# A two-layer attention network on one core: the first layer's attention probabilities transposed in three blocks across heads instead of four, one per head

## The chip, the cores and the metric

The kernel runs on one NeuronCore of a Trainium2 chip. The metric is the device time of one execution in microseconds (us); the median of three runs of the kernel before is 2927.92 us (2922.82 to 2928.58). TensorE is called PE, VectorE DVE, ScalarE ACT, GpSimd POOL and SyncE SP, as in the profile.

## What is computed

Two layers, each a cross attention followed by a feed-forward part, on x of 8 batches x 512 tokens x 512 features. The change touches only the attention of the first layer:

```python
# x: (8, 512, 512), ctx_1024: (8, 77, 512); 16 heads of 32 features
q = (layernorm(x) @ Wq + bq)          # heads of 32
k = (ctx @ Wk + bk)
v = (ctx @ Wv + bv)
scores = einsum('bqhd,bkhd->bhqk', q, k) / sqrt(32)
scores = where(mask, -1e9, scores)
probs  = softmax(scores, axis=-1)     # over the 77 keys
ctx    = einsum('bhqk,bkhd->bqhd', probs, v)
x = x + ctx @ Wo + bo
```

Every product of the attention is made in float32 accuracy from two float32r parts: a matrix is split in a high part (rounded to float32r by ACT) and a low part (the rest, by DVE), and a product is hi x hi + lo x hi + hi x lo, three matmuls into one PSUM bank (`product`, lines 117 to 121).

## The kernel before

The program is a sequence of stages: the first layer (`build_layer0`, to about 680 us), its slots and latents, the second layer's attention, and its experts. Only `build_layer0` is changed.

In it, a **group** s is 4 heads (HC = 4, 128 features) of one batch: s = 4b + c, with c from 0 to 3 (C = 4), so there are G = 32 groups. Batch b has 512 tokens, NT = 4 tiles of 128. The order of work is written by hand: each engine has its own loop over steps s, and engines meet only through semaphores (`pe_s`, `act_s`, `dve_s`, `pool_s`; `mark` counts, `after` waits), so each engine works strictly in its written order. The PSUM banks are placed by the table `place` (line 347), and `claim` (line 353) makes PE wait until the last reader of a bank's former unit has marked it free.

Step s of PE's loop (lines 644 to 691), in this order:

- `scores(s+1, tiles 0 to 2)`: per tile three float32r matmuls of 312 columns and one for the mask (line 571). The scores of tile t go to bank (4s + t) % 3, so tile 3 goes to the bank of tile 0 and waits for DVE to have read that one (`shift`, line 869)
- `probabilities(s, 0)` and `(s, 1)`: the normalised probabilities of one head, 128 tokens x 77 keys, are transposed tile by tile (line 611), four transposes per head into one bank, 77 rows x 512 tokens
- `scores(s+1, tile 3)`, then `queries(s+2)`: 12 matmuls
- `read_out(s, 0)`, `probabilities(s, 2)`, `read_out(s, 1)`, `probabilities(s, 3)`: a read-out is the product of one head's values (stationary) with its transposed probabilities (moving, 512 columns), three matmuls
- work of other batches, by c: c = 0 two tiles of `output(b-1)` (24 matmuls) and `logits(b-2)`; c = 1 the other two tiles of `output(b-1)` and 16 transposes of the next batch's x (line 558); c = 2 `weights_and_sums(b-2)` and 16 transposes for the feed-forward part; c = 3 `hidden(b-1)` (24 matmuls)
- `read_out(s, 2)`, `read_out(s, 3)`

The four read-outs of a group accumulate in one bank (bank 5). The values lie in `Vd`, which is zero but for the head's own 32 columns: head n reads columns n*(P-HD) to n*(P-HD)+128, so that each head adds only to its own 32 output rows. SP fills `Vd` in `values(s)` (lines 385 to 391): 4 heads x 2 parts = 8 DMAs of 77 rows x 32 columns. `values` is called for the groups 0 to 3 before SP's loop, and in step s for group s-1+C once the read-outs of group s-1 are done. `keys(b)` (line 378) loads the keys in 8 DMAs. In the step c = 1 SP also loads the x of batch b+2 into `xa` (line 432); the first such load comes right behind the four calls of `values` ahead of the loop.

ACT copies each transposed head's high part (`probabilities_hi`, line 714), DVE makes its low part (`probabilities_lo`, line 853, recorded at line 805), both of 77 rows x 512. `PT` holds two (high, low) pairs of buffers, and the transposes alternate between banks 3 and 4.

DVE's step (lines 872 to 982) is: `maximum` and `shift` of the four score tiles of s+1 with the low parts of the output of s-1 and of the heads 0 and 1 between them, the low part of the queries, the row sums (line 907, after ACT's exp) and their reciprocal, `probabilities_lo` of heads 2 and 3, and then by c: c = 0 low parts for and work on the routing logits (lines 916, 923, 950 to 962); c = 1 the residual of two output tiles (923), the low parts of the next batch's x, the routing weights (931 to 939) and the statistics; c = 2 low parts for the feed-forward; c = 3 `measure` of the next batch's x, which waits for the DMA into `xa` (line 979). POOL multiplies all of a group's exponentials by their reciprocals at once (line 508).

## Time and profile before

| | |
|---|---|
| median of three runs | 2927.92 us (2922.82 to 2928.58) |
| the profiled execution | 2931.27 us |
| its span | 2929.5 us |
| mean granted clock | 0.957 |
| PE busy | 2664.5 us, 91% |
| DVE busy | 2036.7 us, 70% |
| ACT busy | 1532.9 us, 52% |
| POOL busy | 1522.8 us, 52% |
| from 180 to 560 us: PE, DVE, ACT, POOL busy of 380 | 363.7, 293.0, 160.8, 195.1 us |

The profile is one execution, 1.8 us shorter in its span than in its own time and 3.4 us above the median. The time of a matmul in it includes a modelled end that overlaps the next one, so what a matmul costs in a row of them is read from start to start. A value in brackets behind a row is the idle time of the engine before it and what ended it.

### The profile page before, as it was taken

The numbers are of one execution on the slowest core, as the hardware profiler recorded it, in microseconds if no ns is written. First come the engines' busy times: TensorE is split into PE (matmuls) and PEld (weight loads), VectorE is DVE, ScalarE is ACT, GpSimd is POOL, SyncE is SP. The second block draws the span as 40 slices with busy tenths as digits, with TensorE's granted clock in tenths as the row PEclk, the third lists the DMA queues.
The fourth block names the chain that finished last, engine by engine and source line by source line (L and its number), as shares of the span: only waits on it lengthen the run. The fifth ranks groups of instructions, "written<-read, shape, count | busy, mean of one in ns | idle before, by whom it ended". The sixth has DMA issues, their size and how long they took to land. (4 is left out here: it accounts for less than half of the span.)

```text
span 2929.5 us, 41389 instructions
## 1 busy us (share of the span) xinstructions
PE 2664.5 (91%) x14790; PEld 2217.7 (76%) x14790; DVE 2036.7 (70%) x4037; ACT 1532.9 (52%) x2929; POOL 1522.8 (52%) x1149
## 2 busy tenths in 40 slices
PE   6799999986778699999999999999999999799698
PEld 5687887863435588888888888888888887677476
DVE  3677777742546377777777777777777777577656
ACT  2344344421213377777777777777777777111175
POOL 2355544320000166666666666666666666465555
PEclk9899999997888799999999999999999999899899
DMA  5222222123348633334333243332433314668475
GB/s 186 57 54 56 56 56 57 41 95 128 115 154 316 226 79 81 109 76 121 78 79 110 76 121 78 79 110 75 121 78 79 108 51 135 207 240 282 158 277 186
DMA packets 211758, 351.15 MB, mean 120 GB/s; under 512 B 75071, under 2 KB 81602, under 8 KB 203863
## 3 DMA queue, kind: packets, MB, share of 16 engines
q1 hardware_dynamic: 192771, 284.88, 32.7%
q0 software_dynamic: 11680, 45.02, 4.1%
q10 hardware_dynamic: 7104, 18.61, 1.6%
q8 instruction: 118, 1.93, 0.3%
q14 instruction: 85, 0.70, 0.1%
HBM read 172.47 MB, written 156.64 MB: 112 GB/s over the span
## 5 line engine op out<-in xcount | busy, mean ns | idle before, releaser
L1873 POOL TENSOR_SCALAR pa_Pr<-pa_Pr,pa_rs 128x590 f32<-128x590 f32 x512 | 902.0, 1768 | 487.7 <-DVE pa_rs L2102 487.5
L2106 DVE TENSOR_REDUCE pa_least<-pa_S 128x1 f32<-128x590 f32 x512 | 390.4, 762 | 230.6 <-PE pa_S L1937 228.5
L2027 ACT ACTIVATE pa_Pr<-pa_S,pa_least 128x590 f32<-128x590 f32 x512 | 385.0, 752 | 99.4 <-DVE pa_least L2106 96.2
L2059 DVE TENSOR_TENSOR pa_PTl<-pa_W,pa_PTh 128x512 fp32r<-128x512 f32 (+1 forms) x640 | 420.9, 683 | 20.3 <-ACT pa_PTh L1998 16.0
L1998 ACT ACTIVATE pa_PTh<-pa_W 128x512 fp32r<-128x512 f32 (+1 forms) x640 | 366.6, 595 | 59.2 <-PE pa_W L1948 47.6
L1948 PE MATMUL pa_W<-pa_ident,pa_Pr 128*128 128x128 f32 (+1 forms) x2560 | 370.8, 276 | 0.6
L1948 PEld LDWEIGHTS pa_W<-pa_ident,pa_Pr 128*128 128x128 f32 (+1 forms) x2560 | 303.3, 142 | 30.5 <-POOL pa_Pr L1873 2.9
L1964 PE MATMUL pa_O<-pa_PTh,pa_V 128*128 128x512 f32 (+1 forms) x640 | 289.5, 452 | 17.1 <-DVE pa_PTl L2059 12.8
L1965 PE MATMUL pa_O<-pa_PTl,pa_V 128*128 128x512 f32 (+1 forms) x640 | 253.2, 396 | 0.0
L1935 PE MATMUL pa_S<-pa_U,pa_Qh 128*128 128x296 f32 (+1 forms) x1024 | 228.8, 305 | 7.4 <-ACT pa_Pr L2027 0.4
L1935 PEld LDWEIGHTS pa_S<-pa_U,pa_Qh 128*128 128x128 f32 x1024 | 183.2, 188 | 55.4 <-ACT pa_Pr L2027 21.2
L1937 PE MATMUL pa_S<-pa_Um,pa_Ql 128*128 128x296 f32 (+1 forms) x1024 | 222.9, 299 | 0.0
L508 POOL TENSOR_TENSOR l_E<-l_E,l_rs 128x1232 f32<-128x1232 f32 x32 | 84.7, 2646 | 200.9 <-DVE l_rs L909 200.9
L1937 PEld LDWEIGHTS pa_S<-pa_Um,pa_Ql 128*128 128x128 f32 x1024 | 166.4, 189 | 0.0
L1964 PEld LDWEIGHTS pa_O<-pa_PTh,pa_V 128*128 128x128 f32 (+1 forms) x640 | 121.4, 190 | 44.2 <-DVE pa_PTl L2059 35.4
L119 PE MATMUL pa_W<-Wkv_hi,pa_z_hi 128*128 128x256 f32 x512 | 144.7, 283 | 0.0
L121 PE MATMUL pa_W<-Wkv_hi,pa_z_lo 128*128 128x256 f32 x512 | 144.2, 282 | 0.0
L120 PE MATMUL pa_W<-Wkv_lo,pa_z_hi 128*128 128x256 f32 x512 | 144.1, 281 | 0.0
L2553 ACT ACTIVATE ex_xT_hi<-ex_bank 128x512 fp32r<-128x512 f32 x92 | 53.0, 599 | 142.2 <-PE ex_bank L2449 135.9
L1965 PEld LDWEIGHTS pa_O<-pa_PTl,pa_V 128*128 128x128 f32 (+1 forms) x640 | 123.0, 192 | 5.2
L119 PE MATMUL pa_W<-pa_z_hi,Wq_hi 128*128 128x512 f32 x256 | 107.2, 419 | 18.6 <-DMA pa_z_lo<-z_s 18.6
L1998 ACT ACTIVATE pa_U<-pa_W 64x512 fp32r<-64x512 f32 x128 | 75.7, 592 | 90.1 <-PE pa_W L121 88.5
(503 smaller groups left out, 6647.5 us busy)
## 6 DMA issues: line engine op xcount, KB each, us to landing
xs_s<-pa_Ql SPq DMA_DIRECT2D x57, 576.0 KB
pa_Um<-pa_U SPq DMA_DIRECT2D x128, 147.5 KB
pa_Qh<-pa_Qh SPq DMA_DIRECT2D x128, 128.0 KB
o_s<-pa_O_hi SPq DMA_DIRECT2D x64, 256.0 KB, 2.0
o_s<-pa_O_lo SPq DMA_DIRECT2D x64, 256.0 KB, 2.3
Wkv_hi<-o_s SPq DMA_DIRECT2D x8, 2048.0 KB, 11.2
Wkv_lo<-o_s SPq DMA_DIRECT2D x8, 2048.0 KB, 16.7
l_xa<-x SPq DMA_DIRECT2D x8, 1024.0 KB, 6.4
```

The lines of the kernel that those rows point to most:

```text
L119: pe.matmul(out, a[0], b[0], start=first, stop=False)
L121: return pe.matmul(out, a[1], b[0], start=False, stop=last)
L1873: pool.tensor_scalar(p, p, rs[:, g % 2, t:t + 1], None, ALU.mult).then_inc(*pool_s.mark("probs", n))
L1935: pe.matmul(out[:, a0:a1], qh, U[p % 2][x][:, a0:a1], start=True, stop=False)
L1937: m = pe.matmul(out[:, a0:a1], ql, Um[p % 2][x][:, a0:a1], start=False, stop=True)
L1948: m = pe.transpose(bank_of[u][0:KEYS[c], t * P:(t + 1) * P], Pr[g % 2][:, t, c * P:c * P + KEYS[c]], ident[:, :])
L1964: pe.matmul(Oc[:, :], v, PTh[0:n, r, :], start=(c == 0), stop=False)
L1965: pe.matmul(Oc[:, :], v, PTl[0:n, r, :], start=False, stop=(c == NC - 1)).then_inc(*pe_s.mark("PV", g, c))
L1998: act.activation(out, src, ACT.Copy, scale=scale).then_inc(*act_s.mark("hi", *name))
L2027: act.activation(Pr[g % 2][:, t, :], scored[n % 2], ACT.Exp, scale=-1.0, bias=least[:, g % 2, t:t + 1], accum_out=rs[:, g % 2, t:t + 1]).t ...
L2059: dve.tensor_tensor(out, src, f32(hi_ap), ALU.subtract).then_inc(*dve_s.mark(*name))
L2106: dve.tensor_reduce(least[:, g % 2, t:t + 1], scored[n % 2], AX, ALU.min).then_inc(*dve_s.mark("least", n))
```

## The change

The probabilities of a group lie in SBUF as 4 heads x 77 keys = 308 adjacent columns per token tile. They are now cut without regard to heads into NK = 3 blocks of 128, 128 and 52 columns (`ROWS`). `PT` of a block has 128 (or 52) rows, and the values in `Vd` are laid out to match: row r of block k is key column 128k + r, and holds the 32 values of its head in that head's columns, zeros elsewhere. A read-out covers a block, not a head. So `values` has to cut the heads at the block edges: `pieces` has 6 parts (77, 51, 26, 77, 25 and 52 rows). The third block has two matmuls in place of three: its low part is written by DVE to rows 64 to 115 under the high part in rows 0 to 51 of the same buffer, and the high values are loaded a second time for these rows, so that one product of 116 rows makes hi x hi + hi x lo. `turn` alternates buffers and banks over three blocks per group.

```diff
-    VW = HC * P - (P - HD)
+    KEYS = HC * SK
+    NK = -(-KEYS // P)
+    ROWS = [min(P, KEYS - k * P) for k in range(NK)]
+    VW = NK * P
...
+        edges = sorted({n * SK for n in range(HC + 1)} | {k * P for k in range(NK)})
+        pieces = [(e // P, e % P, e // SK, e % SK, e1 - e) for e, e1 in zip(edges, edges[1:])]
+        turn = lambda s, n: (NK * s + n) % 2
+        TWIN = P // 2
+        loads = [(z, k, r0 + up, n, s0, r) for z in range(2) for k, r0, n, s0, r in pieces for up in ((0, TWIN) if (z, k) == (0, NK - 1) else (0,))]
...
             def values(s):
                 b, c = divmod(s, C)
-                for z in range(2):
-                    for n in range(HC):
-                        d = c * P + n * HD
-                        sp.dma_start(f32(Vd[z][0:SK, c, n * P:n * P + HD]),
-                                     V_s[z][b * SK:(b + 1) * SK, d:d + HD]).then_inc(vd_in[c], 16)
+                for z, k, r0, n, s0, r in loads:
+                    d = n * HD
+                    sp.dma_start(f32(Vd[z][r0:r0 + r, c, k * P + d:k * P + d + HD]),
+                                 V_s[z][b * SK + s0:b * SK + s0 + r, c * P + d:c * P + d + HD]).then_inc(vd_in[c], 16)
...
                 for t in range(NT):
-                    m = pe.transpose(ps[0:SK, t * P:(t + 1) * P], E[s % 2][:, t, n, :], ident[:, :])
+                    m = pe.transpose(ps[0:ROWS[n], t * P:(t + 1) * P], both[:, s % 2, t * KEYS + n * P:t * KEYS + n * P + ROWS[n]], ident[:, :])
...
                 pe.wait_ge(*dve_s.after("free", "PT", s, n))
-                w = n * (P - HD)
-                product(pe, bank_of["O", s][:, :], [z[:, c, w:w + P] for z in Vd], [z[:, :] for z in PT[n % 2]],
-                        n == 0, n == HC - 1).then_inc(*pe_s.mark("PV", s, n))
+                r, out, p = ROWS[n], bank_of["O", s][:, :], PT[turn(s, n)]
+                v = [z[:, c, n * P:(n + 1) * P] for z in Vd]
+                if n < NK - 1:
+                    last = product(pe, out, v, [z[:, :] for z in p], n == 0, False)
+                else:
+                    pe.matmul(out, v[0][0:TWIN + r, :], p[0][0:TWIN + r, :], start=False, stop=False)
+                    last = pe.matmul(out, v[1][0:r, :], p[0][0:r, :], start=False, stop=True)
+                last.then_inc(*pe_s.mark("PV", s, n))
...
                 if group(s):
-                    for n in range(2):
-                        read_out(s, n)
-                        probabilities(s, n + 2)
+                    read_out(s, 0)
+                    probabilities(s, 2)
+                    read_out(s, 1)
...
                 if group(s):
-                    for n in range(2, HC):
+                    for n in range(2, NK):
                         read_out(s, n)
...
             def probabilities_lo(s, n):
-                lo_of(PT[n % 2][1][0:SK, :], bank_of["PT", s, n][0:SK, :], PT[n % 2][0][0:SK, :], "PT", s, n)
+                r, i = ROWS[n], turn(s, n)
+                low = PT[i][1][0:r, :] if n < NK - 1 else PT[i][0][TWIN:TWIN + r, :]
+                lo_of(low, bank_of["PT", s, n][0:r, :], PT[i][0][0:r, :], "PT", s, n)
```

ACT's `probabilities_hi` and the loops of ACT and DVE over heads 2 and 3 now run over the blocks from 2 to NK, which is block 2 alone; waits on the last head now wait on the last block.

PE, the end of step 0 (group 0, no work of other batches), before: behind the query products the read-outs of heads 0 to 3 (`l_PT`, `l_Vd`) with the transposes of heads 2 and 3 (`l_E`) between them, up to the scores of the next group (`l_Kd`).

```order
244 L121 MATMUL l_bank<-l_PT,l_Vd_lo 128x512
245 L611 MATMUL l_bank<-l_ident,l_E 77x128 [waits l0_dve]
246 L611 MATMUL l_bank<-l_ident,l_E 77x128 x3
247 L119 MATMUL l_bank<-l_PT,l_Vd_hi 128x512 [waits l0_dve]
248 L120 MATMUL l_bank<-l_PT,l_Vd_hi 128x512
249 L121 MATMUL l_bank<-l_PT,l_Vd_lo 128x512
250 L611 MATMUL l_bank<-l_ident,l_E 77x128 [waits l0_dve]
251 L611 MATMUL l_bank<-l_ident,l_E 77x128 x3
252 L119 MATMUL l_bank<-l_PT,l_Vd_hi 128x512 [waits l0_dve]
...
255 L119 MATMUL l_bank<-l_PT,l_Vd_hi 128x512 [waits l0_dve]
...
258 L119 MATMUL l_bank<-l_Kd_hi,l_qT_hi 128x312 [waits l0_dve]
```

The same place in the changed kernel:

```order
244 L121 MATMUL l_bank<-l_PT,l_Vd_lo 128x512
245 L618 MATMUL l_bank<-l_ident,l_E 52x128 [waits l0_dve]
246 L618 MATMUL l_bank<-l_ident,l_E 52x128 x3
247 L119 MATMUL l_bank<-l_PT,l_Vd_hi 128x512 [waits l0_dve]
248 L120 MATMUL l_bank<-l_PT,l_Vd_hi 128x512
249 L121 MATMUL l_bank<-l_PT,l_Vd_lo 128x512
250 L632 MATMUL l_bank<-l_PT,l_Vd_hi 128x512 [waits l0_dve]
251 L633 MATMUL l_bank<-l_PT,l_Vd_lo 128x512
252 L119 MATMUL l_bank<-l_Kd_hi,l_qT_hi 128x312 [waits l0_dve]
```

The fourth set of transposes is gone from between the second read-out and the work of other batches, and one whole read-out and one matmul are gone from behind that work.

SP, ahead of its loop, before: one call of `values` (two rows) stands four times between the load of x into `l_x` and the load of the second batch into `l_xa`.

```order
19 L405 DMA l_x<-x 128x4x512
20 L390 DMA l_Vd_hi<-V_s 77x32 x4
21 L390 DMA l_Vd_lo<-V_s 77x32 x4
...
28 L432 DMA l_xa<-x 128x4x512
```

And in the changed kernel, of which one of the four calls is shown:

```order
19 L412 DMA l_x<-x 128x4x512
20 L397 DMA l_Vd_hi<-V_s 77x32
21 L397 DMA l_Vd_hi<-V_s 51x32
22 L397 DMA l_Vd_hi<-V_s 26x32
23 L397 DMA l_Vd_hi<-V_s 77x32
24 L397 DMA l_Vd_hi<-V_s 25x32
25 L397 DMA l_Vd_hi<-V_s 52x32 x2
26 L397 DMA l_Vd_lo<-V_s 77x32
...
68 L439 DMA l_xa<-x 128x4x512
```

A call has 13 DMAs where it had 8, and the load into `l_xa` now stands behind 52 of them where it stood behind 32.

## Rows read from the trace of the kernel before

**Rows 1.** The page's first line, then busy times of one long stretch of the first layer
```profile
span 2929.5 us, 41389 instructions
...
180.00:560.00 380.00, 363.73 (x1984) 301.85 (x1983) 292.96 (x625) 160.84 (x254) 195.14 (x112) 0.99 0.22 61
```

**Rows 2.** PE's timeline (start us, us): transposes and products of one group, c = 0 and 3
```profile
358.07 0.60 PE L611 MATMUL l_bank<-l_ident,l_E 128*77 128x128 f32 x4
358.42 0.48 PE L119 MATMUL l_bank<-l_Wo_hi,l_oT_hi 128*128 128x512 f32 x1
358.74 0.40 PE L120 MATMUL l_bank<-l_Wo_lo,l_oT_hi 128*128 128x512 f32 x1
...
348.90 0.39 PE L119 MATMUL l_bank<-l_PT,l_Vd_hi 128*128 128x512 f32 x1
...
350.29 0.31 PE L119 MATMUL l_bank<-l_Kd_hi,l_qT_hi 128*128 128x312 f32 x1
```

**Rows 3.** PE's timeline: transposes of 77 columns, then of 128, each with its follower
```profile
352.00 1.03 PE L611 MATMUL l_bank<-l_ident,l_E 128*77 128x128 f32 x8
352.79 0.39 PE L119 MATMUL l_bank<-l_Kd_hi,l_qT_hi 128*128 128x312 f32 x1
...
311.63 1.91 PE L558 MATMUL l_bank<-l_ident,l_xa 128*128 128x128 f32 x16
313.30 0.47 PE L119 MATMUL l_bank<-l_PT,l_Vd_hi 128*128 128x512 f32 x1
```

**Rows 4.** Groups of the whole trace by shape: a second-layer product that contracts 77 rows
```profile
L1964 PE MATMUL pa_O<-pa_PTh,pa_V 77*128 77x512 f32 x128 | 52.2, 408 | 0.9 <-DVE pa_PTl L2059 0.4
```

**Rows 5.** From c = 1 to c = 2: DVE, then PE, then PE's such waits from 180 to 560 us
```profile
311.83 0.69 DVE L923 TENSOR_TENSOR l_x<-l_bank,l_x 128x512 f32<-128x512 f32 x1 [2.12 <-PE l_bank L121]
...
319.54 0.38 PE L119 MATMUL l_bank<-l_Kd_hi,l_qT_hi 128*128 128x312 f32 x1 [2.01 <-DVE l_E L869]
...
PE l_bank L119 <- DVE l_E L869: 10.1, 6, 2.0
```

**Rows 6.** From c = 0 to c = 1: DVE (two rows), then PE
```profile
366.91 0.42 DVE L950 TENSOR_TENSOR l_router<-l_bank,l_b_bc 128x256 f32<-128x256 f32 x1 [0.59 <-PE l_bank L121]
...
370.10 0.48 DVE L869 TENSOR_TENSOR l_E<-l_bank,l_mx 128x308 f32<-128x308 f32 x1
...
370.72 0.38 PE L119 MATMUL l_bank<-l_Kd_hi,l_qT_hi 128*128 128x312 f32 x1
```

**Rows 7.** From c = 2 to c = 3: DVE (two rows), then PE
```profile
332.21 2.48 DVE L805 TENSOR_TENSOR l_fT_lo<-l_bank,l_fT_hi 128x512 fp32r<-128x512 f32 x4 [2.54 <-ACT l_fT_hi L697]
...
335.38 0.48 DVE L869 TENSOR_TENSOR l_E<-l_bank,l_mx 128x308 f32<-128x308 f32 x1
...
336.60 0.39 PE L119 MATMUL l_bank<-l_Kd_hi,l_qT_hi 128*128 128x312 f32 x1
```

**Rows 8.** PE in the first batch (group 3), at `read_out(s, 2)`
```profile
145.09 0.50 PE L119 MATMUL l_bank<-l_PT,l_Vd_hi 128*128 128x512 f32 x1 [1.93 <-DVE l_PT L805]
```

**Rows 9.** Ahead of SP's loop: SP's first issues of values and the load behind them; DVE; PE
```profile
76.60 1.56 SPq L390 DMA_DIRECT2D l_Vd_hi<-V_s  x4
...
89.29 0.39 SPq L432 DMA_DIRECT2D l_xa<-x  x1
...
94.69 2.47 DVE L812 BATCH_NORM_STATS2 l_stats<-l_xa 128x6 f32<-128x512 f32 x4 [5.75 <-DMA l_xa<-x]
...
98.67 0.60 PE L119 MATMUL l_bank<-l_Kd_hi,l_qT_hi 128*128 128x312 f32 x1 [5.57 <-DVE l_E L869]
```

**Rows 10.** SP's own waits from 60 to 600 us (us in total, times, longest)
```profile
SPq L390 <- PE l_bank L121: 223.5, 28, 20.6
```

**Rows 11.** Clock: a stretch behind the wait of rows 5 (PEclk is third from the end), and PE in it
```profile
318.00:328.00 10.00, 8.46 (x36) 6.64 (x37) 7.91 (x19) 3.47 (x7) 9.13 (x6) 0.83 0.63 185
...
321.15 0.63 PE L119 MATMUL l_bank<-l_xT_hi,l_Wq_hi 128*128 128x512 f32 x1
321.58 0.63 PE L120 MATMUL l_bank<-l_xT_lo,l_Wq_hi 128*128 128x512 f32 x1
```

More of the change, by code:

```diff
@@ L420, in _ @@
                 if s == G:
-                    sp.wait_ge(*pe_s.after("PT", G - 1, HC - 1))
+                    sp.wait_ge(*pe_s.after("PT", G - 1, NK - 1))
                     hidden_weights(1)
@@ L426, in _ @@
                 if group(s - 1) and group(s - 1 + C):
-                    sp.wait_ge(*pe_s.after("PV", s - 1, HC - 1))
+                    sp.wait_ge(*pe_s.after("PV", s - 1, NK - 1))
                     values(s - 1 + C)
@@ L714, in probabilities_hi @@
             def probabilities_hi(s, n):
[L715 removed]
+                hi_of(PT[turn(s, n)][0][0:ROWS[n], :], bank_of["PT", s, n][0:ROWS[n], :], "PT", s, n)
             for s in steps:
@@ L724, in _ @@
                     d = (s - 1) % C
-                    act.wait_ge(*pe_s.after("PV", s - 1, HC - 1))
+                    act.wait_ge(*pe_s.after("PV", s - 1, NK - 1))
                     act.activation(oT[0][:, (s - 1) % OS, :], bank_of["O", s - 1][:, :], ACT.Identity,
@@ L751, in _ @@
                 if group(s):
-                    probabilities_hi(s, 2)
-                    probabilities_hi(s, 3)
+                    for n in range(2, NK):
+                        probabilities_hi(s, n)
                 if c == 1 and batch(b + 1):
@@ L910, in _ @@
                 if group(s):
-                    probabilities_lo(s, 2)
-                    probabilities_lo(s, 3)
+                    for n in range(2, NK):
+                        probabilities_lo(s, n)
                 if c == 0 and batch(b - 2):
```

5 lines of the change are left out of this document (2 added, 3 removed).

## The prediction

> **What bounds the kernel now.** I read four views, in this order. The busy times by stretch come first: from 180 to 560 us, 22 groups of the first layer, PE is busy 363.7 of 380 us and DVE 293.0 [rows 1]. So PE's issue sets the pace there, one group in 17.3 us, and a matmul that is taken from PE is worth its spacing, unless PE then arrives early at something late. PE's timeline comes second, because the spacing and not the duration is what a matmul costs, and because it shows where PE already stands still. Third are the timelines of DVE at these places, to see what DVE itself waited for: if it waited for PE, its chain starts at a PE instruction and keeps its length, and what PE saves behind that instruction becomes a longer wait. Fourth is SP's queue, since the change gives SP more DMAs.
>
> **What PE saves in one group.** Removed are four transposes and four products of 512 columns.
> - The fourth set of transposes takes from 358.07 to 358.42, 0.35 us, and the product behind it needs 0.32 us to its follower where others need 0.23 to 0.24 [rows 2]. With this 0.08, 0.43 us. It stands ahead of the other batches' work.
> - Six products of read-outs take from 348.90 to 350.29, 0.232 us each [rows 2]. Four of them go, 0.93 us, all behind the other batches' work.
> - That the last block contracts 116 and 52 rows changes nothing: a product over 77 rows takes 408 ns [rows 4], and those over 128 take 390 to 480 [rows 2].
> Together 1.36 us; for 32 groups 43.5 us.
>
> **What of it is lost to waits.** The other side is always DVE's.
> - c = 1 to 2. PE waits 2.01 us for DVE to free the bank of score tile 0. DVE's chain (residual, four low parts, weights, statistics, maximum, shift) begins behind a 2.12 us wait for PE's last output product [rows 5]; PE's read-outs lie in parallel with it, and the 0.93 us they save go into this wait. Six such waits total 10.1 us from 180 to 560 us [rows 5], a seventh follows: 7 x 0.93 = 6.5 us.
> - c = 0 to 1. No wait shows, but DVE's shift ends at 370.58 and PE begins at 370.72 [rows 6]: the slack is used up. DVE's chain again starts behind a wait for PE (0.59 us, the logits) [rows 6]. It occurs for batches 2 to 7: 6 x 0.93 = 5.6 us, as a new wait at the same line.
> - c = 2 to 3. The low parts end at 334.69 (332.21 + 2.48), maximum and shift take one us more, PE comes at 336.60 [rows 7], now at 335.67. About 0.15 behind the shift's end it would be 335.84, so 0.17 is lost, six times; in the last batch, where the same low parts delay the transposed probabilities, I take 0.6. Together 1.6 us.
> - c = 3 to 0: DVE waits for PE in every batch, nothing is lost.
> - First batch. There is nothing between the read-outs, and PE waits 1.93 us for the low part of the third head [rows 8], whose chain starts at the end of the queries. The 0.43 us of transposes lie inside this wait: 4 x 0.43, with 0.3 for its c = 1 boundary, 2.0 us. In batch 1 POOL's normalisation delays PE at c = 2; 0.4 us.
> - Wider transposes. Eight of 77 columns take 0.79 us, sixteen of 128 take 1.67 [rows 3]: 0.099 against 0.104 each, so 0.05 us per group for the eight wide ones, some 1.0 us where PE is not waiting anyway.
> The losses are 17.1 us, and 26.4 us remain.
>
> **ACT and DVE** lose one copy and one low part per group. They hide under PE and are costed at nothing; were they ever on the path, it would be a gain. The low part of the last block is written 64 partitions below its source. The trace has no such instruction; between its neighbours' price and twice that, it is covered, because DVE has just lost a whole one and then waits for PE.
>
> **SP.** Each call of `values` has 13 DMAs in place of 8. In the loop this is hidden: SP stands 223.5 us in 28 waits for PE ahead of these loads [rows 10], and the values are used three steps later. If that cover went, five issues of 0.396 us would cost 2.0 us in each of 28 groups. Ahead of the loop it is not hidden. 32 issues take from 76.60 to 89.29, 0.396 us each, and the load of the second batch into `xa` is issued at once behind them. It lands at 94.69, where DVE has waited 5.75 us for it in `measure`, and behind `measure` stand the maxima for which PE waits 5.57 us [rows 9]. So SP's queue is the path, from its first load to PE. Twenty more issues at 0.396 are 7.9 us, late for everything that follows. The bounds are 1.0, if issue goes by rows moved (668 per call where there were 616: 8% of 12.7 us, about 1.0), and 9.2, if the load of `xa`, 5.4 us from issue to DVE's start [rows 9], is slowed by a quarter among more small DMAs as well. I take 7.9: the 1 MB load of `xa` itself is issued in 0.39 us [rows 9], as long as a 9.6 KB one, so an issue goes by the instruction, not by size.
>
> The Trainium skill (DMA: Bandwidth & Descriptors, "Issuing engines are not separate DMA queues") says that the sequencer's time to start a DMA is usually small beside the DMA itself. By it the 7.9 us would be near nothing and the sum 23.2 us. I keep the trace's spacing, for 32 issues in a row without a wait show SP, not the transfers, as what delays the load.
>
> **The clock.** After the 2.01 us wait the granted clock of 318 to 328 us is 0.83, and products are 0.43 us apart (321.15 to 321.58) [rows 11], not 0.23: the lower level, 1.2 GHz, for eight products, 1.6 us lost. Of the six waits in the long stretch two are followed by this. The waits grow to about 2.9 us and six new ones of some 0.9 us come. I take two more such stretches, 3.2 us; the bounds are none and eight (12.8 us).
>
> **Sum.** 43.5 - 17.1 - 7.9 - 3.2 = 15.3 us less. The profiled span of 2929.5 becomes 2914.2 and its own time, 2931.3, becomes 2916.0; against the median, 3.4 us lower, that is 2912.6 us.
>
> **Rivals.**
> 1. SP's issues are hidden, or short DMAs issue faster. For it: short rows, little data. Against: 0.396 us steady over 32. With the lower bound of 1.0 for SP it gives 26.4 - 1.0 - 3.2 = 22.2 us, 2905.7 us. Chance 0.12.
> 2. The waits do not grow, since DVE also sheds a low part per group (0.6 us) and starts its chains earlier. Against: these chains start behind waits for PE. It gives 43.5 - 1 - 7.9 = 34.6 us, 2893.3 us. Chance 0.09.
> 3. Slower than before: the clock. Each grown or new wait drops PE to 1.2 GHz behind it, at the c = 1 and c = 0 boundaries (13) and in the first batch (4): 17 x 1.6 = 27.2 us against 18.5, so 8.7 us slower, 2936.6 us. It decides from 12 such stretches on (12 x 1.6 = 19.2). Against: four of six waits of 2 us had no such follower. Chance 0.04. The Trainium skill (TensorE: Matmul & The Clock Gate, "HAM oscillation — how this bites in real kernels") describes a kernel that falls back to the low clock in every idle gap between its bursts; by this rule this rival would be the rule here. Two of six in this trace agree with it and four do not.
> 4. The change does not take PE's work away, for instance because the two matmuls of the last block cost more than others, or the load after the widened issue lands late also in the loop. Then some 26 us of gain fall to a few, and the time is within 0.2%. Chance 0.07.
>
> **How the numbers follow.** The forecast has the remaining 0.68. Its own range: with eight clock stretches and 9.2 for SP it is 26.4 - 9.2 - 12.8 = 4.4 us, 2923.5; with none and 7.9 it is 18.5 us, 2909.4. To hold 8 in 10 the range reaches down over rival 1, to 2901, and leaves out rivals 2 and 3: 2901 to 2923. A measurement of this kernel tells 0.2%, 5.9 us, from no change. Rivals 1 and 2 and nearly all of the forecast lie beyond: faster 0.87, same 0.09 (rival 4 and the slow end of the forecast), slower 0.04.
>
> **What would show it.** In the profile after: 12 transposes and 8 products per group (384 and 256 in all); SP's 52 issues ahead of `xa` lasting 20.6 us, with DVE's wait for it near 13.6 us and PE's near 13.5; in the later batches a wait of some 2.9 us at c = 1 and a new one near 0.9 at c = 0, both for line L869's successor; four groups taking some 3.4 us less than before. If PE's waits stay at 2 us, rival 2 holds; if the first batch starts on time, rival 1. The prediction is wrong in its reason if the time between the first group and the last falls by less than 20 or more than 30 us.

## The result, and the profile after

The changed kernel takes 2941.57 us (median of 14 runs, 2933.32 to 2951.82), the kernel before on the same chip 2931.57 (14 runs, 2922.82 to 2936.9). The ratio is 1.0036, 95% interval 1.0026 to 1.0046: some 10 us slower, where 15 us less had been forecast, and outside the forecast's range. The profiled execution of the changed kernel is its fastest one (2933.32 us, span 2931.5), 2.0 us longer than the one before. The loss is in its trace all the same: the first layer takes 11.6 us more (the column "layer" further down), and the parts of the program ahead of it and behind it, which nobody changed, happened to take 9.6 us less.

PE is busy for a shorter time, as predicted, and the layer still takes longer. The page's first line and the stretch of [rows 1] in the changed kernel (us; busy of PE, PEld, DVE, ACT, POOL with counts; granted clock, share of DMA, GB/s):

```profile
span 2931.5 us, 40973 instructions
...
180.00:560.00 380.00, 352.43 (x1779) 284.06 (x1778) 290.69 (x601) 144.67 (x227) 181.97 (x111) 0.94 0.23 61
```

The granted clock is 0.94 where it was 0.99. The groups of the whole trace by shape (busy us, mean ns, idle before them):

```profile
L618 PE MATMUL l_bank<-l_ident,l_E 128*128 128x128 f32 x256 | 39.3, 305 | 2.6 <-POOL l_E L515 2.6
...
L618 PE MATMUL l_bank<-l_ident,l_E 128*52 128x128 f32 x128 | 19.2, 272 | 0.0
...
L633 PE MATMUL l_bank<-l_PT,l_Vd_lo 52*128 52x512 f32 x32 | 17.7, 552 | 0.0
L632 PE MATMUL l_bank<-l_PT,l_Vd_hi 116*128 116x512 f32 x32 | 15.9, 495 | 8.4 <-DVE l_PT L817 8.4
```

384 transposes are there, 12 per group, and with the six products of the first two blocks 8 products per group. But those over 52 rows have a mean of 552 ns, where the 77-row product of [rows 4] has 408 (part of that is the lower clock described below). PE's timeline at the end of a group (start us, us):

```profile
359.52 0.40 PE L632 MATMUL l_bank<-l_PT,l_Vd_hi 116*128 116x512 f32 x1
359.85 0.50 PE L633 MATMUL l_bank<-l_PT,l_Vd_lo 52*128 52x512 f32 x1
360.28 0.41 PE L119 MATMUL l_bank<-l_Kd_hi,l_qT_hi 128*128 128x312 f32 x1
360.53 0.30 PE L120 MATMUL l_bank<-l_Kd_lo,l_qT_hi 128*128 128x312 f32 x1
```

Read from start to start: 0.33, 0.43 and 0.25 us. In the kernel before the same three steps (two products and the first scores) take 0.23, 0.23 and 0.14 (0.15 at the place shown):

```profile
349.83 0.40 PE L120 MATMUL l_bank<-l_PT,l_Vd_hi 128*128 128x512 f32 x1
350.06 0.39 PE L121 MATMUL l_bank<-l_PT,l_Vd_lo 128*128 128x512 f32 x1
350.29 0.31 PE L119 MATMUL l_bank<-l_Kd_hi,l_qT_hi 128*128 128x312 f32 x1
350.44 0.31 PE L120 MATMUL l_bank<-l_Kd_lo,l_qT_hi 128*128 128x312 f32 x1
```

So 0.41 us of the 1.36 saved per group are gone at once, before and behind the 52-row matmul.

Ahead of SP's loop, SP, DVE and PE (to be read beside [rows 9]):

```profile
73.99 2.54 SPq L397 DMA_DIRECT2D l_Vd_hi<-V_s  x7
...
93.60 0.40 SPq L439 DMA_DIRECT2D l_xa<-x  x1
...
98.81 2.47 DVE L824 BATCH_NORM_STATS2 l_stats<-l_xa 128x6 f32<-128x512 f32 x4 [12.48 <-DMA l_xa<-x]
...
102.79 0.60 PE L119 MATMUL l_bank<-l_Kd_hi,l_qT_hi 128*128 128x312 f32 x1 [12.29 <-DVE l_E L883]
```

52 issues take 19.6 us, DVE waits 12.5 and PE 12.3: this is what was forecast (20.6, 13.6 and 13.5), a little smaller.

What had not been foreseen stands at c = 0. PE's waits from 180 to 560 us (us in total, times, longest):

```profile
PE l_bank L119 <- DVE l_E L883: 12.1, 6, 2.8
PE l_bank L119 <- DVE l_hTs_lo L930: 6.1, 5, 1.2
```

The first is the wait at c = 1 to 2, 12.1 us where [rows 5] had 10.1. (One of the six in [rows 5] is only 0.48 us long, that of the first such boundary in the stretch; the other five are 1.8 to 2.0.) The second is new: the logits wait for the low parts of the router's hidden features, in every batch from 2 on. DVE and POOL at such a place, in the kernel before:

```profile
361.17 0.25 DVE L909 RECIPROCAL l_rs<-l_rs 128x16 f32<-128x16 f32 x1
361.34 1.22 DVE L805 TENSOR_TENSOR l_PT<-l_bank,l_PT 77x512 fp32r<-77x512 f32 x2
362.48 1.28 DVE L916 TENSOR_TENSOR l_hTs_lo<-l_hT,l_hTs_hi 128x512 fp32r<-128x512 f32 x2
...
361.51 4.36 POOL L508 TENSOR_TENSOR l_E<-l_E,l_rs 128x1232 f32<-128x1232 f32 x1 [2.90 <-DVE l_rs L909]
```

and in the changed kernel, with PE's wait:

```profile
371.28 0.25 DVE L923 RECIPROCAL l_rs<-l_rs 128x16 f32<-128x16 f32 x1
371.56 0.68 DVE L817 TENSOR_TENSOR l_PT<-l_bank,l_PT 52x512 fp32r<-52x512 f32 x1
372.28 2.74 DVE L930 TENSOR_TENSOR l_hTs_lo<-l_hT,l_hTs_hi 128x512 fp32r<-128x512 f32 x2
...
371.62 2.25 POOL L515 TENSOR_TENSOR l_E<-l_E,l_rs 128x1232 f32<-128x1232 f32 x1 [2.24 <-DVE l_rs L923]
...
375.16 0.27 PE L119 MATMUL l_bank<-l_W_hi,l_hTs_hi 128*128 128x64 f32 x1 [1.21 <-DVE l_hTs_lo L930]
```

The pair of low parts reads two operands from SBUF, and POOL's normalisation reads and writes SBUF. Before, POOL gave way: 4.36 us, and DVE's pair took 1.28. POOL ended 2.11 us behind the end of DVE's pair (361.51 + 4.36 against 362.48 + 1.28), almost as long as the 2.25 us that the whole normalisation takes in the changed kernel: it got hardly anything done until DVE's unbroken run of instructions was over. Now POOL takes 2.25 and DVE's pair 2.74, and PE waits for DVE. There is a small difference ahead of it: before, each DVE instruction starts 0.08 us ahead of the end of the one before it (361.34 against 361.17 + 0.25 = 361.42; 362.48 against 362.56); now 0.03 to 0.04 us behind it (371.56 against 371.53; 372.28 against 372.24).

Behind PE's wait the clock falls, at all six such places; in the kernel before it stays at 1.00 at all six. The 20 us around the same place of one batch, before and after (columns as above):

```profile
286.00:306.00 20.00, 20.00 (x119) 17.42 (x117) 16.20 (x40) 8.38 (x12) 6.49 (x3) 1.00 0.03 6
```

```profile
298.00:318.00 20.00, 18.78 (x82) 16.17 (x81) 15.50 (x35) 2.88 (x6) 2.25 (x1) 0.74 0.03 5
```

In this batch the 24 logit matmuls take from 303.28 to 307.49, 4.2 us, where they took 2.6, and the scores behind them are 0.26 us apart and not 0.14.

### The profile page after: what moved, and what is told of

It is laid out like the page before. It is cut to its first block and busy times, and to the rows that moved or that the text cites. A ratio compares the mean times of both kernels' runs of the same rounds, so it can differ in the third digit from the quotient of the medians.

```text
span 2931.5 us, 40973 instructions
## 1 busy us (share of the span) xinstructions
PE 2648.6 (90%) x14534; PEld 2191.9 (75%) x14534; DVE 2034.5 (69%) x4005; ACT 1517.1 (52%) x2897; POOL 1511.3 (52%) x1149
## 5 line engine op out<-in xcount | busy, mean ns | idle before, releaser
L515 POOL TENSOR_TENSOR l_E<-l_E,l_rs 128x1232 f32<-128x1232 f32 x32 | 72.0, 2250 | 227.2 <-DVE l_rs L923 227.1
```

## The experiments

Every ratio is to the kernel before, run beside it on the same chip. Its median was 2931.6 us in the comparison with the changed kernel, 2932.4 beside a1 to a4, 2932.8 beside b1 to b4, 2933.9 beside c1 to c4 and 2931.8 beside d1 and d2; microseconds are worked out from the ratios and 2931.6. A difference between two of the runs below is uncertain by 4 to 8 us, going by their intervals (some 5 for most pairs). "Layer" is the time in the profiled execution from SP's first load of values to the first transposes of the slots' stage; "clock" is the granted clock from 180 to 560 us. The profiled execution can lie off its median: that of a4 is its slowest, that of a1 its second fastest.

| run | median us | ratio, 95% interval | layer | clock |
|---|---|---|---|---|
| before | 2931.6 | 1 | 613.9 | 0.99 |
| changed | 2941.6 | 1.0036 (1.0026 to 1.0046) | 625.5 | 0.94 |
| a1_full_rows | 2927.7 | 1.0000 (0.9985 to 1.0015) | 609.0 | 0.98 |
| a2_early_x | 2931.6 | 0.9999 (0.9986 to 1.0012) | 616.6 | 0.95 |
| a3_low_part_twice | 2942.1 | 1.0034 (1.0021 to 1.0047) | 621.6 | 0.96 |
| a4_router_low_earlier | 2921.6 | 0.9965 (0.9953 to 0.9977) | 607.4 | 0.98 |
| b1_no_twin | 2916.1 | 0.9945 (0.9932 to 0.9958) | 600.5 | 0.98 |
| b2_before_52_rows | 2940.6 | 1.0036 (1.0023 to 1.0049) | 624.1 | 1.00 |
| b3_all_three | 2905.9 | 0.9921 (0.9908 to 0.9934) | 590.0 | 0.99 |
| b4_before_two_edits | 2925.9 | 0.9980 (0.9971 to 0.9990) | 610.5 | 0.99 |
| c1_no_twin_gap | 2934.7 | 1.0005 (0.9991 to 1.0019) | 612.5 | 0.97 |
| c2_late_block_1 | 2954.6 | 1.0082 (1.0058 to 1.0106) | 639.4 | 0.92 |
| c3_before_13_loads | 2939.5 | 1.0023 (1.0008 to 1.0037) | 618.6 | 0.99 |
| c4_no_twin_two_edits | 2907.4 | 0.9915 (0.9893 to 0.9937) | 589.3 | 0.98 |
| d1_shift_alone | 2935.8 | 1.0010 (0.9998 to 1.0022) | 617.3 | 0.96 |
| d2_before_gap | 2948.3 | 1.0054 (1.0037 to 1.0072) | 627.6 | 0.98 |

### The 52-row matmul

a1_full_rows, the changed kernel with

```diff
-                    last = pe.matmul(out, v[1][0:r, :], p[0][0:r, :], start=False, stop=True)
+                    last = pe.matmul(out, v[1], p[0][:, :], start=False, stop=True)
```

> The changed kernel, whose last block's second matmul reads all 128 rows of the values' low part in place of 52 (the further rows of the values are zeros, so the sum is the same); nothing else moves. Theory A (a matmul over 52 rows between matmuls over 128 costs PE some 0.4 to 0.6 us in each of 32 groups, since PE changes the size of its tile and back): in the trace the three steps from the last block's first matmul to the scores behind it take 0.6 to 0.65 us where they took 1.0 at c = 3, and the time falls by 8 to 18 us, from 2941.6 to about 2929, ratio to the kernel before 0.996 to 1.001. Rival B (52 rows are harmless and the gaps in the trace are modelled ends; the time went into SP, waits and clock): spacing and time stay, 2939 to 2944 us, ratio 1.003 to 1.004.

Measured 1.0000: 10.5 us less than the changed kernel (0.0036 of 2931.6; 14.7 by the medians), and theory A holds. The steps are 0.24, 0.23 and 0.14 us again:

```profile
348.68 0.39 PE L632 MATMUL l_bank<-l_PT,l_Vd_hi 116*128 116x512 f32 x1
348.92 0.39 PE L633 MATMUL l_bank<-l_PT,l_Vd_lo 128*128 128x512 f32 x1
349.15 0.30 PE L119 MATMUL l_bank<-l_Kd_hi,l_qT_hi 128*128 128x312 f32 x1
349.29 0.31 PE L120 MATMUL l_bank<-l_Kd_lo,l_qT_hi 128*128 128x312 f32 x1
```

Not all of this gain is the matmul's own: PE's waits at the logits are still 1.2 us each, and yet the clock went up from 0.94 to 0.98. b2 puts the price of the matmul alone on the kernel before:

```diff
-                product(pe, bank_of["O", s][:, :], [z[:, c, w:w + P] for z in Vd], [z[:, :] for z in PT[n % 2]],
-                        n == 0, n == HC - 1).then_inc(*pe_s.mark("PV", s, n))
...
+                    last = pe.matmul(out, v[1][0:52, :], p[0][0:52, :], start=False, stop=True)
```

(the last head's third matmul alone; the others are as they were).

> The kernel before, with one edit: the third matmul of the last head's read-out (low part of the values) reads rows 0 to 51 in place of all 128. It leaves out keys 52 to 76 of that head in that one low term. Nothing else changes, so it is the price of a 52-row matmul by itself. Theory A: 0.4 to 0.6 us more per group where PE isn't waiting, and PE's waits for DVE at c = 1 take up to 7 groups' worth: 25 x 0.5 = 12 us slower, range 8 to 20, ratio 1.003 to 1.007. If the longer steps also bring the low clock, up to 25 us. Rival B: no difference beyond 3 us, ratio 0.999 to 1.001.

Measured 1.0036, 10.5 us (7.8 by the medians; the layer 10.2 us longer). PE's timeline there:

```profile
212.27 0.39 PE L626 MATMUL l_bank<-l_PT,l_Vd_hi 128*128 128x512 f32 x1
212.59 0.49 PE L627 MATMUL l_bank<-l_PT,l_Vd_lo 52*128 52x512 f32 x1
213.01 0.41 PE L119 MATMUL l_bank<-l_Kd_hi,l_qT_hi 128*128 128x312 f32 x1
213.26 0.31 PE L120 MATMUL l_bank<-l_Kd_lo,l_qT_hi 128*128 128x312 f32 x1
```

0.32, 0.42 and 0.25 us, and the same within 0.02 at all 25 such places from 180 to 600 us. 32 times 0.41 would be 13 us; some 3 us of it lie inside waits (PE's wait at c = 1 to 2 is 1.6 us in place of 2.0, in seven batches). The clock stays at 1.00, so the matmul costs by itself and does not bring the low clock by itself. The Trainium skill (TensorEngine Tiling (Array Packing), "Key Properties") says that a change of the tiling mode drains TensorE. The steps before and behind the 52-row matmul would agree with that; that contracting 52 rows is such a change is not shown. Other row counts don't show the steps: the step from a 128-row product into a 116-row one is 0.23 us (a1), and those into and out of the 77-row products of [rows 4] are 0.23 and 0.23 to 0.24.

### SP's queue

a2_early_x, the changed kernel with the load moved ahead (the one in the loop is then left out for this batch):

```diff
             sp.wait_ge(cleared, 4)
+            sp.wait_ge(*pe_s.after("xT", 0, C - 1))
+            sp.dma_start(xa[:, :, :], whole_x(a["x"], 1)).then_inc(xa_in, 16)
             for s in range(C):
                 values(s)
```

> The changed kernel, with SP's load of the second batch's x put ahead of the 52 loads of values in place of behind them. Theory (SP's queue is the path ahead of the loop): DVE's wait for that load falls from 12 us to less than 1, PE's first wait of 12.3 us falls to a few us or becomes a wait for the values, and the time falls by 7 to 12 us against the changed kernel, to 2930 to 2935 us, ratio to the kernel before 0.9995 to 1.001. Rival (the values are needed as early, so PE waits for them instead, or the statistics of the second batch are not what the scores wait for): the first wait shrinks by less than 3 us and the time with it, 2938.5 us or more.

Measured 0.9999, some 11 us less than the changed kernel; PE's wait of 12.3 us and DVE's of 12.5 are gone. (The 2.6 us in which PE waits for POOL's normalisation just ahead stand in every version.) The edit takes away also what the kernel before had paid there (5.6 us of PE's wait), as b4, which has the same edit, shows below. The price of the added issues alone is c3, the kernel before with 13 loads per group:

```diff
+                        cuts = (0, 51, SK) if HC * z + n < 5 else (0, SK)
+                        for s0, s1 in zip(cuts, cuts[1:]):
...
```

> The kernel before with 13 DMAs per group of values in place of 8 (five of the eight are cut in two at row 51), and nothing else: the price of SP's issues by itself. Theory (0.39 us per issue, SP's queue is the path ahead of the loop, hidden in it): PE's first wait goes from 5.6 to 12 or 13 us, nothing changes in the loop, 7 to 8 us slower: 2939 to 2941 us, ratio 1.002 to 1.0033. Rival 1 of the prediction (issues hidden): 2931 to 2934 us, ratio within 0.001 of 1.

Measured 1.0023, 6.7 us (5.6 by the medians; the layer 4.7 us longer). DVE's wait for the load is 10.0 us where it was 5.8, PE's first wait 10.4 where it was 5.6, behind 52 issues in 18.4 us, and PE's waits in the loop are as before. The term of the forecast (7.9 us) was of the right kind and a little too large: the issues are 0.35 us apart here and 0.38 in the changed kernel, not 0.396.

### DVE's low parts and POOL

The first idea was that DVE, with one low part less ahead, came to the router's low parts too early. a3 put 0.7 us back:

```diff
+                if n == NK - 1 and s % C == 0 and batch(s // C - 2):
+                    dve.wait_ge(*act_s.after("hi", "PT", s, n))
+                    dve.tensor_tensor(low, bank_of["PT", s, n][0:r, :], f32(PT[i][0][0:r, :]), ALU.subtract).then_inc(padded, 1)
+                    dve.wait_ge(padded, s // C - 1)
```

> The changed kernel, in which DVE writes the last block's low part twice at c = 0 of the batches 2 to 7 (the same numbers to the same place), so that the low parts of the router's hidden features begin some 0.7 us later, where they began in the kernel before. Theory C (there the low parts and POOL's normalisation, both reading and writing SBUF alone, met in another order, and DVE's pair of low parts took 2.74 us in place of 1.28; the logits then come 1.2 us late and PE goes to 1.2 GHz behind them): the pair takes 1.3 to 1.5 us again, POOL's normalisation 4 us, PE's wait at the logits goes, the low-clock stretches behind them become fewer, and the time falls by 5 to 15 us, 2927 to 2937 us, ratio 0.9985 to 1.002. Rival D (the meeting does not depend on 0.7 us, or the logits are as late by the added instruction; the low clock comes from something else): time within 3 us of the changed kernel, 2939 to 2944 us, with the same low-clock stretches behind c = 0.

Measured 1.0034: a miss. The pair takes 2.0 us, POOL 2.25, PE's wait stays 1.2 us. The number of low parts ahead is not what decides. (Both of them are written 64 rows further down here, with the gaps around them.) a4 moved the pair out of POOL's way:

```diff
+                if c == 0 and batch(b - 2):
+                    for j in range(J):
+                        dve.wait_ge(*act_s.after("hhi", b - 2, j))
+                        dve.tensor_tensor(hTs[1][:, j, :], hT[:, j, :], f32(hTs[0][:, j, :]), ALU.subtract)\
+                           .then_inc(*dve_s.mark("hlo", b - 2, j))
                 if new:
                     e = (s + 1) % 2
...
-                if c == 0 and batch(b - 2):
...
```

> The changed kernel, in which DVE makes the two low parts of the router's hidden features at c = 0 ahead of its wait for ACT's exp (1.8 us idle) in place of behind the last block's low part. Theory C: PE's wait at the logits (1.2 us in each of six batches) goes, and with it the low clock of the 8 to 10 us behind c = 0 (8 transposes at 1.46 us in place of 0.80, products 0.43 us apart): the time falls by 8 to 18 us, 2924 to 2934 us, ratio 0.997 to 1.001. Rival D (low clock from the 52-row matmul or by chance): the wait at the logits goes, but the low-clock stretches stay; the time falls by 3 to 7 us only, since DVE's chain then ends at the same wait of PE's for the logits, 2935 to 2939 us.

Measured 0.9965, 20.8 us less than the changed kernel, a little more than theory C had. The six waits were 7.3 us of it. At the places behind the logits, PE spends 6.8 us at the lower clock in place of 37.4; at half the speed these 30.6 us are worth up to 15.3 us. Against both, a new wait of 0.33 us comes at c = 0 to 1 in four batches. Two stretches of low clock behind the logits stayed (at 501 and 569 us, without a wait ahead of them).

What decides is shown by b1, c1 and d1. b1 reads the last block out as the others and has no low part under the high one:

```diff
-                    pe.matmul(out, v[0][0:TWIN + r, :], p[0][0:TWIN + r, :], start=False, stop=False)
-                    last = pe.matmul(out, v[1][0:r, :], p[0][0:r, :], start=False, stop=True)
+                last = product(pe, out, v, [z[:, :] for z in p], n == 0, n == NK - 1)
...
-                low = PT[i][1][0:r, :] if n < NK - 1 else PT[i][0][TWIN:TWIN + r, :]
+                low = PT[i][1][0:r, :]
```

> Three blocks as in the changed kernel, but the last block read out as the others: three matmuls over all 128 rows (the values are zero beyond row 52), its low part in a buffer of its own in rows 0 to 51, no second load of the high values (12 DMAs per call). It gives back one matmul of 0.23 us per group (7.4 us in all) and takes away both the 52-row matmul and the low part written 64 rows below its source. Theory A (the 52-row matmul costs 0.4 to 0.6 us per group): PE's steps at the last block are 0.23 each, the time is 2921 to 2932, ratio 0.997 to 1.000. Theory C2 (DVE's low part that shifts rows starts only when the instruction before it has ended, and so POOL's normalisation gets ahead of DVE's low parts of the router's features): the pair of these takes 1.3 us again and POOL's normalisation 4.4, and PE's wait of 1.2 us at the logits is gone. If the pair still takes over 2 us with this kernel, C2 falls and it is the low part that is missing that lets them meet. Rival B (the gain went to SP, waits and clock whatever the last block is): 2941 or more, ratio 1.003 or more.

Measured 0.9945, 16.1 us faster than the kernel before, with one matmul per group more and one load per call less than the changed kernel. DVE and POOL at c = 0:

```profile
354.45 0.25 DVE L919 RECIPROCAL l_rs<-l_rs 128x16 f32<-128x16 f32 x1
354.62 0.62 DVE L813 TENSOR_TENSOR l_PT<-l_bank,l_PT 52x512 fp32r<-52x512 f32 x1
355.16 1.27 DVE L926 TENSOR_TENSOR l_hTs_lo<-l_hT,l_hTs_hi 128x512 fp32r<-128x512 f32 x2
...
354.78 3.76 POOL L515 TENSOR_TENSOR l_E<-l_E,l_rs 128x1232 f32<-128x1232 f32 x1 [2.39 <-DVE l_rs L919]
```

The instructions overlap by 0.08 us again, the low part takes 0.62 us and not 0.68, and it is POOL that gives way. c1 adds to b1 nothing but the gap:

```diff
+                    if c == 0 and batch(b - 2) and new:
+                        dve.wait_ge(*dve_s.after("rsum", s + 1))
                     for n in range(2, NK):
                         probabilities_lo(s, n)
+                    if c == 0 and batch(b - 2):
+                        dve.wait_ge(*dve_s.after("free", "PT", s, NK - 1))
```

> The kernel b1 (three blocks, the last read out with three full matmuls, no shifted low part; 2916.1 us, ratio 0.9945) with two waits added on DVE at c = 0: the last block's low part starts when the reciprocal has ended, and the router's low parts when the last block's low part has ended. In b1 these overlap by 0.08 us each, as in the kernel before. Nothing is waited for that isn't over 0.1 us later anyway. Theory C2 (who holds SBUF is decided by whether DVE's instructions follow each other without a gap): the router's pair takes 2.7 us in place of 1.27, POOL's normalisation 2.25 in place of 3.8, PE waits 1.2 us at the logits in six batches, and with the low clock behind it the time is 8 to 18 us more: 2924 to 2934 us, ratio 0.997 to 1.0005. Rival (it is where the low part is written, or the missing instruction, that matters): pair and time as in b1, 2914 to 2919 us.

Measured 1.0005 against 0.9945, 17.6 us for two waits that move DVE by some 0.1 us each in six batches (the last row is PE's wait from 180 to 560 us):

```profile
358.50 0.25 DVE L919 RECIPROCAL l_rs<-l_rs 128x16 f32<-128x16 f32 x1
358.78 0.68 DVE L813 TENSOR_TENSOR l_PT<-l_bank,l_PT 52x512 fp32r<-52x512 f32 x1
359.50 2.73 DVE L930 TENSOR_TENSOR l_hTs_lo<-l_hT,l_hTs_hi 128x512 fp32r<-128x512 f32 x2
...
358.83 2.25 POOL L515 TENSOR_TENSOR l_E<-l_E,l_rs 128x1232 f32<-128x1232 f32 x1 [2.38 <-DVE l_rs L919]
...
PE l_bank L119 <- DVE l_hTs_lo L930: 6.1, 5, 1.2
```

d1 asks why the changed kernel has the gap. It is b1 with the low part written 64 rows further down in its own buffer (PE reads the old rows, so the last block's low part is missing from the result):

```diff
-                low = PT[i][1][0:r, :]
+                low = PT[i][1][0:r, :] if n < NK - 1 else PT[i][1][TWIN:TWIN + r, :]
```

> The kernel b1 (three full matmuls for the last block; 2916.1 us, ratio 0.9945) with one edit: DVE writes the last block's low part to rows 64 to 115 of its own buffer in place of rows 0 to 51. PE reads the same rows as in b1, so the last block's low part is missing from the result, and nothing but the place of that write changes. Theory C2a (the move to other partitions is what keeps DVE's instruction from overlapping its neighbours, and the gap hands SBUF to POOL): the low part takes 0.68 us in place of 0.62 and stands 0.04 us apart from its neighbours, the router's pair takes 2.7 us, PE waits 1.2 us at the logits, and the time is that of c1, 2928 to 2936 us, ratio 0.998 to 1.001. Rival C2b (the changed kernel's gap comes from the low part lying in the buffer of the high part that it reads): low part, pair and time as in b1, 2914 to 2919 us.

Measured 1.0010, 19 us more than b1 by the ratios, and PE waits 7.3 us at the logits in six waits:

```profile
357.69 0.25 DVE L919 RECIPROCAL l_rs<-l_rs 128x16 f32<-128x16 f32 x1
357.98 0.69 DVE L813 TENSOR_TENSOR l_PT<-l_bank,l_PT 52x512 fp32r<-52x512 f32 x1
358.69 2.74 DVE L926 TENSOR_TENSOR l_hTs_lo<-l_hT,l_hTs_hi 128x512 fp32r<-128x512 f32 x2
...
358.03 2.25 POOL L515 TENSOR_TENSOR l_E<-l_E,l_rs 128x1232 f32<-128x1232 f32 x1 [2.07 <-DVE l_rs L919]
```

So the write to other partitions is enough to make the gap; that it shares the buffer with the high part is not needed. d2 adds c1's two waits to the kernel before.

> The kernel before, with the two waits of c1 on DVE at c = 0 (each for something that is over within 0.1 us). Theory C2: the router's low parts take 2.0 to 2.7 us in place of 1.28, POOL's normalisation 2.3 in place of 4.4. PE comes to the logits 0.43 us later than in c1, so its wait there is 0 to 0.8 us, and the six read-out products behind the logits keep the clock up: 2933 to 2940 us, ratio 1.000 to 1.003. Rival (the gap matters only with the last block's short low part): pair 1.3 us, time within 2 us of the kernel before.

Measured 1.0054, 15.8 us, nearly twice the upper end of what I expected. The wait at the logits is 0.8 us, the upper end of the expected, but the clock falls behind it in all six batches, even with six products of 512 columns to follow. PE's timeline, with rows left out:

```profile
294.90 0.27 PE L119 MATMUL l_bank<-l_W_hi,l_hTs_hi 128*128 128x64 f32 x1 [0.78 <-DVE l_hTs_lo L920]
...
297.57 0.65 PE L119 MATMUL l_bank<-l_PT,l_Vd_hi 128*128 128x512 f32 x1
298.03 0.63 PE L120 MATMUL l_bank<-l_PT,l_Vd_hi 128*128 128x512 f32 x1
298.45 0.63 PE L121 MATMUL l_bank<-l_PT,l_Vd_lo 128*128 128x512 f32 x1
```

They are 0.42 to 0.46 us apart: 1.2 GHz. From the first output product of that batch to the end of the next group's first scores PE takes 14.1 us (from 288.3) where the kernel before takes 11.5 (from 427.6 in its batch): 0.9 of the 2.6 lies ahead of the logits, 1.6 behind them.

c2 tried to keep the clock up in the changed kernel by putting the read-out of block 1 behind the logits:

```diff
-                    read_out(s, 1)
+                    if c != 0:
+                        read_out(s, 1)
...
-                    for n in range(2, NK):
+                    for n in range(1 if c == 0 else 2, NK):
```

> The changed kernel, in which at c = 0 the read-out of block 1 stands behind the work of other batches in place of ahead of it, so that behind the logits (96 matmuls of 64 columns) PE has five matmuls of 512 columns ahead of the scores where the changed kernel has two and the kernel before six. Theory (the low clock behind the logits comes from what PE does around them): the low-clock stretches at c = 0 become fewer (six in the changed kernel); the wait at the logits grows by 0.7 us to 1.9, since PE comes to it earlier. 6 times 5 us of low clock at half speed are at most 15 us; less 6 x 0 for the wait, since the new cover stands behind it: 2928 to 2938 us, ratio 0.999 to 1.0025. Rival: the clock falls because of the wait of 1.2 us and the 52-row matmul; the wait becomes longer, the stretches stay, 2940 to 2946 us, ratio 1.003 to 1.005.

(There are 24 matmuls of 64 columns at the logits, not 96.) Measured 1.0082, a miss worse than its rival: PE comes earlier to the logits and waits 1.9 us there, and the clock is 0.92. More products behind the logits didn't keep the clock; taking away the wait ahead of them did, in most batches (a4).

The granted clock of the 12 us behind PE's first logit product, at the six places of each trace, puts the runs in order:

| wait at the logits | 52-row matmul | run: places with a clock under 1.00, time at 1.2 GHz in all six |
|---|---|---|
| none | none | before, b1, b3, b4, c3: 0 of 6; c4: 1 of 6, 3.4 us |
| none | yes | b2: 0 of 6; a4: 2 of 6, 6.8 us |
| 1.2 us | none | a1: 3 of 6, 20 us; c1: 3 of 6, 20 us; d1: 5 of 6, 31 us |
| 1.2 us | yes | changed: 6 of 6, 37 us; a2: 6 of 6, 31 us; a3: 5 of 6, 27 us |
| 0.8 us | none | d2: 6 of 6, 20 us |
| 1.9 us | yes | c2: 6 of 6, 54 us |

So the wait is what mainly brings the low clock. The 52-row matmul without a wait brings little or none of it; with the wait it may add some (a1 against the changed kernel), but one trace of each does not settle how much.

### The versions that beat both

b3 is a1, a2 and a4 together.

> The changed kernel with three edits together: all 128 rows in the last matmul, the second batch's x loaded ahead of the values, and the router's low parts made ahead of the wait for ACT's exp. If their gains (about 13, 10 and 20 us by the single runs against 2941.6) add up fully: 2899 us, ratio 0.989. If the clock is shared between the first and the third (each took away most of the low stretches behind c = 0), the gain is less than the sum: 2905 to 2912 us, ratio 0.991 to 0.9935. I expect the latter. Above 2920 the edits stand in each other's way.

Measured 0.9921: 23 us faster than the kernel before. The single gains (10.5, 10.8 and 20.8 us, 42.1 together) don't add up, as expected: b3 is 33.7 us faster than the changed kernel. b4 gives the two edits that need no change to the kernel before.

> The kernel before (four heads) with the two edits that do not need the change: the second batch's x loaded ahead of the values, and the router's low parts made earlier. It tells what the change itself is worth beside b3. Expected: DVE's wait of 5.8 us for the load goes and with it PE's wait of 5.6 us (4 to 6 us); the earlier low parts bring nothing, since PE doesn't wait at the logits here: 2924 to 2929 us, ratio 0.998 to 0.9995. If it is as fast as the kernel with all three edits, the three blocks are worth nothing even without their side effects.

Measured 0.9980, 5.9 us faster. So with the side effects gone the three blocks are worth 17.3 us (0.9921 against 0.9980; some 5 us either way). c4 has b1's read-out and the same two edits.

> Three blocks, the last read out with three full matmuls and an unshifted low part (b1), with the second batch's x loaded ahead of the values and the router's low parts made earlier. Against b3 (2905.9 us) it has 0.23 us more of matmul per group (7.4 us) and none of the shifted low part, whose collision b3 avoids by the moved low parts. If the twin is worth its matmul once both side effects are taken away, this one is slower than b3: 2908 to 2914 us, ratio 0.993 to 0.995. If it is as fast or faster (2906 or less), putting the low rows under the high rows brings nothing here.

Measured 0.9915, against 0.9921 for b3, with intervals that overlap. The low rows under the high rows save a matmul of 0.23 us per group, 7.4 us in all, and no gain can be seen: c4 is 1.8 us faster by the ratios, uncertain by some 8 us, and the layer takes 589.3 us in its trace and 590.0 in that of b3.

## Why the prediction was wrong, by its steps

- **PE's saving, 1.36 us per group.** The instructions went as said. The failed step is the sentence "That the last block contracts 116 and 52 rows changes nothing": 116 rows change nothing, 52 rows cost 0.41 us of steps per group, 13 us of the 43.5. Rival 4 had named this cost. The row that it rested on has 77 rows; it was the nearest but no bound, since nothing in the trace had fewer. b2 shows 10.5 us for it alone.
- **"costed at nothing", the shifted low part.** This step failed too. Its own length was bounded well (0.68 us for 0.62) and it is covered, but the bounds asked only for its duration. What it does to its neighbour was not asked: two gaps of 0.03 us in place of two overlaps of 0.08 let POOL have SBUF first. d1 against b1: 19 us by the ratios, 16.8 in the layer. 7.3 us are PE's new waits; d1 spends 31 us behind the logits at the lower clock and b1 none, which is worth up to 15 us and covers the rest.
- **SP, 7.9 us.** Right in mechanism and place; c3 has 6.7 by its ratio, and PE's first wait grew by 6.7 us in the changed kernel and by 4.8 in c3. Reading the Trainium skill (DMA: Bandwidth & Descriptors, "Issuing engines are not separate DMA queues") as the prediction did, the cost would have been near nothing; the runs decide for the rows.
- **The waits at c = 1 to 2.** They grew by 2.0 us from 180 to 560 where 5.6 were forecast (and two waits of 0.7 us came a few us ahead of them, in the batches in which they did not grow). The new wait at c = 0 to 1 (5.6 us forecast) does not show in the changed kernel, where PE is late from the logits. Where that lateness is gone it shows, with less than the 0.93 us forecast: 0.33 us in four batches of a4, 0.40 to 0.47 in all six of b1, 0.40 to 0.72 in all six of b3. The first batch's waits are near the forecast (2.5 us in place of 1.9, where 0.43 more had been put). Whether 17.1 us of losses were too many or too few, the runs can't tell. For b1 the forecast's own terms give 43.5 - 7.4 - 17.1 - 6.3 - 3.2 = 9.5 us (one matmul more, 16 issues more), and 16.1 were measured; for c4 against b4 43.5 - 7.4 - 17.1 - 3.2 = 15.8, measured 19.1; but for b3 against b4 43.5 - 17.1 - 3.2 = 23.2, measured 17.3.
- **The clock, 3.2 us.** Mis-sized for the changed kernel: 0.94 against 0.99 of 380 us is up to 19 us, while PE works. The count that it rested on was off as well: of the six waits in the stretch one is 0.48 us, so two of five waits near 2 us were followed by the low clock, not two of six. Rival 3 had this cost, but at other places: it put the stretches behind grown waits at c = 1, new ones at the first scores after c = 0, and in the first batch. They came behind the logits. It had a chance of 0.04; rival 4, two matmuls of the last block that cost more than others, had 0.07. Both were in part what happened, together with a third effect that no rival named.
- **"What would show it".** The test on the time between the first and the last group was the right one: from PE's first scores behind the wait of the prologue to the slots it rose by 4.8 us (591.8 to 596.7) in place of falling by 20 to 30. In b1 it falls by 18.5.

What the parts of the change are worth, each by the run that isolates it: the blocks with full matmuls and an unshifted low part 16.1 us faster (b1, with 4 issues per call more); the added issues 6.7 us slower (c3); the 52-row matmul 10.5 us slower (b2, and a1); the shifted low part 19 us slower (d1). Added up, 16.1 less 29.5, plus 7.4 for the matmul saved, would be 6 us slower, and 10 were measured; that is within what such a sum of runs can tell.

Left open: how much of its possible 15.3 us the clock is worth in a4, how much the 52-row matmul adds to the low clock where there is a wait, and why in two batches of a4 and one of c4 the clock falls behind the logits without a wait ahead of them.

## To carry to other kernels

A matmul that contracts few rows between matmuls that contract all can cost more than the one it saves (0.41 us of steps against 0.23 here): read the steps into it and out of it, and let it read zero rows if there are any. An engine's instruction that is covered can still change who gets SBUF first; where DVE and POOL both work in SBUF, look whose instruction PE waits for, and move DVE's to where it waits anyway. And a bound from the nearest row holds only for what that row has in common with the new instruction: its duration, here, but not its neighbours.

## What the runs showed of the hardware

- Steps around a 52-row matmul: 0.32 or 0.33, 0.42 or 0.43 and 0.25 us in place of 0.23, 0.23 and 0.14 to 0.15, at all 25 places alike (b2).
- A DVE subtraction whose output lies 64 partitions below its inputs doesn't overlap its neighbours (0.68 us and gaps of 0.03, against 0.62 and overlaps of 0.08 with the same rows: d1, b1). An added wait for the preceding instruction does the same (c1).
- With DVE's instructions overlapped, POOL's multiply gave way though its row begins 0.97 us ahead of DVE's pair (361.51 against 362.48; 4.36 us for 2.25). It ended 2.11 us behind the pair's end, and so it did in b1 (354.78 + 3.76 against 355.16 + 1.27), where DVE's run was one low part shorter. With a gap it kept SBUF, and DVE's first subtraction ended 0.55 us behind POOL's end (2.14 us from 372.28, against 371.62 + 2.25).
- The Trainium skill (SBUF — State Buffer, "SBUF: two separate sides") says that of a POOL instruction that reads SBUF and a DVE one with two SBUF inputs, whichever starts first has the shared ports for its whole instruction. The changed kernel agrees with that. The kernel before does not if one goes by the rows of these two; it would if DVE's overlapped instructions count as one stretch, since that began ahead of POOL (the reciprocal at 361.17). No run separates the two readings.
- A wait of 0.8 us ahead of the logits was followed by 1.2 GHz behind them in six of six batches (d2); a wait of 1.2 us in three to six of six (a1, c1, d1, a2, a3, changed); 52-row matmuls without a wait left the clock at 1.00 (b2).
